# A graph network in twelve stages: steps further apart, byte flags, divided transfers, and two pieces of work in other stages

## The chip, the cores and the metric

The kernel runs on one core of one Trainium2 chip. A core has five engines, each with its own list of instructions: TensorE (PE in the profile; PEld is its loading of weights), VectorE (DVE), ScalarE (ACT), GpSimd (POOL) and SyncE (SP, which here only issues transfers), and sixteen DMA engines. The metric is the device time of one execution in microseconds (us); the profile also gives nanoseconds (ns) for single instructions.

## What is computed

x has 100000 nodes of 128 features; 50000 edges go from `src` (random) to `dst` (sorted). Four layers follow, each with a residual and a layer norm over the features. Cut to what matters:

```python
def _L0(x):     # attention per head (4 heads of 32)
    h = (x @ W).reshape(N, H, C)
    alpha = leaky_relu(s_src[row] + s_dst[col], 0.2)
    m = maximum(segment_max(alpha, row), 0.0); ex = exp(alpha - m[row])
    denom = segment_sum(ex, row) + (E - deg)[:, None] * exp(-m)
    return segment_sum((ex / denom[row])[:, :, None] * h[col], col) + bias
def _L1(x):     # attention over the edges of a receiver
    w = exp(e - m[receiver]);  e = sum(Q[receiver] * K[sender]) * scale
    attn = segment_sum(w * V[sender], receiver) / segment_sum(w, receiver)
    return x + attn @ Wo
def _L2(x):     # two graph convolutions; norm = dinv[dst] * dinv[src], with self loops
    for W, b in ((W0, b0), (W1, b1)):
        x = relu(segment_sum((x @ W)[src] * norm[:, None], dst) + b)
    return x
def _L3(x):     # messages of scalars and vectors; emb: 8 Gaussians of edge_weight
    w = mlp(emb); xs, xv = s @ W_up0, v @ W_up1
    mid = w * combinations(xs[src], xv[src], edge_attr_3 / norm(edge_attr_3))
    return segment_sum(mid, dst) @ W_out / 16
for layer in (_L0, _L1, _L2, _L3):
    x = layernorm(x + layer(x))
```

## The kernel before

`build` calls twelve stages one after the other, with a barrier of all engines between two: `prepare`, `scores_and_sort`, `gat_softmax`, `gat_sums`, `first_layer`, `radial_basis`, `attention_scores`, `attention_softmax`, `second_layer`, `gcn_first`, `gcn_second`, `final_edges`. Most stages run over the edges: 98 items of 4 x 128 edges (`ITEMS`), while `gat_softmax` also runs over all nodes (196 halves). A tile of an item is 128 partitions x 512 numbers; four buffers (`BUFS`) of each tile take turns.

The order of the work is written out by hand. `pipeline(engine, (f, lag), ...)` makes one engine's list: in slot q it does, in the order in which the parts stand, f for item q - lag. The engines aren't tied slot by slot. Each goes on as soon as what it waits for is there; `wait_item(engine, sems, t, u, back)` waits until a buffer of the item `back` earlier is free. A lag thus says how many items lie between two steps in an engine's list.

A sum over the edges of a receiver is made by turning the item with TensorE (edges to the free axis), a running sum along it on VectorE (`tensor_tensor_scan`), which goes on where the flag `cont` is 1 and begins anew where it is 0, and a multiplication by a weight matrix, which turns it back. The last edge of each receiver holds the sum. The scan of an item takes its start from the last column of the one before.

`prepare` loads the ids of the edges and the edge vectors, finds the flags (`same`, L377) and stores them as f32 in `t_cont`; the ids go from SBUF to `t_ids` (L281 to 284) and come back in another layout (L287). Each of the four scanning stages loads the 512 flags of its item for all partitions (`edge_line`, 256 KB).

`gat_softmax` (L937): GpSimd gathers scores (L978), the nodes run through the graph convolution without edges as a pipeline of 196 halves, VectorE then does the softmax over the sources in one go after `SPLIT` = 100 slots (L1088 on), GpSimd scatters the result (L985) while the pipeline goes on. `find_segments` (L860) finds where the segments of a list of ids begin and end; it needs four turns by TensorE (L857), one after the other. It is done for the sources there and for the targets in `gat_sums` (L1145), which then sums the attention over the receivers (`segment_scan`), stores the totals, loads them as rows and turns them. `radial_basis` (L2062) makes the eight Gaussians (`kept_emb`) for all edges from 8 loads of the weights, two VectorE operations, a square and an exponential on ScalarE, and a product.

The stages with loops over items, and their lists:

- `second_layer` (L1583): `weight` (GpSimd, L1629), `turn` (TensorE, L1646), `scan` (L1678), `multiply` (L1653), `add` with the measure of the norm (L1685, L1254 to 1268), `root` (ScalarE, L1277), `scale` (L1287, L1289), `widen` (GpSimd, L1634 to 1637: scale and shift times a factor of the node, for two outputs), `apply` (ScalarE, L1664, L1665), two stores.
- `gcn_first` (L1701) and `gcn_second` (L1795): four indirect gathers on GpSimd (L1724, L1822), `turn` of both the gathered and the own rows (L193, L194), `scan` (L1778, L1882), `multiply` (L1756, L1864; the second with a row of the bias times the degree's root, L1861), `take` or `add`, and the output. The second adds x2, which `second_layer` stored.
- `final_edges` (L1902): four gathers (L1960), `scale_x`, `turn_x`, `copy_x`, `project`, `messages`, `turn_sums`, `scan`, `reduce`, `combine`, `root`, `scale`, `apply`, four scatters to the output (L1952) `SCATTER_LAG` items after the gather.

## Time and profile before

| | |
|---|---|
| median of three runs | 7871.08 us (7854.48 to 7896.73) |
| the profiled execution | 7874.37 us, its span 7872.4 us |
| busy, share of the span | PE 51%, PEld 40%, DVE 45%, ACT 34%, POOL 48% |
| transfers | 1048.5 MB, mean 133 GB/s |
| mean granted TensorE clock | 0.672 of full speed |

The profile is of one execution. Busy times leave out register, branch, semaphore and DMA-issuing instructions, except that an indirect DMA counts on GpSimd, which makes it. A wait is put down to what released it; "issue" is time in which an engine waited for nothing that the profile shows, "remote" is a release whose instruction the profile does not name. The stages end at 94.7, 1384, 3340, 3489, 3897, 3957, 4650, 4686, 5375, 5973, 6590 and 7872 us.

### The profile page before, as it was taken

To read this page: it belongs to the slowest core of one execution; us is meant where nothing else is said; L and a number is where in the kernel's file an instruction comes from. 1 tells how busy PE (TensorE), PEld (TensorE's weight loads), DVE (VectorE), ACT (ScalarE), POOL (GpSimd) and SP (SyncE) were. 2 spreads that over 40 slices of the span, in tenths; PEclk is the share of its full clock that TensorE was granted. 3 is DMA by queue.
4 is the path that set the end of the run, shared out by engine and by line. 5 is a ranking of instruction groups with operands and counts; after the bars stand their busy time and mean duration, and the time that the engine had idled before them with its cause. 6 is when DMAs were issued, how large, how long until landed. Compare 5 with 4: busy or idle time off the path is not lost. (4 is left out here: it accounts for less than half of the span.)

```text
span 7872.4 us, 85274 instructions
## 1 busy us (share of the span) xinstructions
PE 4003.5 (51%) x18822; PEld 3174.7 (40%) x18822; DVE 3570.1 (45%) x12700; ACT 2687.6 (34%) x6766; POOL 3751.2 (48%) x4124
## 2 busy tenths in 40 slices
PE   2444444112961118825468764444556885555555
PEld 1443344101641015514356543333554554555554
DVE  4484444001671005548711135553334665656665
ACT  0014455001861018815433324442222332222222
POOL 3655655775006750003255532225665664666665
PEclk9655555555985559957789975556666666777676
DMA  1236666111851016624455547776777996333333
GB/s 51 64 89 184 185 191 188 36 19 48 262 174 34 21 39 216 216 64 132 110 132 151 158 129 193 190 192 155 178 180 183 220 218 150 98 101 98 101 98 79
DMA packets 1395766, 1048.50 MB, mean 133 GB/s; under 512 B 171017, under 2 KB 1232586, under 8 KB 1395521
## 3 DMA queue, kind: packets, MB, share of 16 engines
q1 hardware_dynamic: 1279294, 866.89, 39.6%
q0 software_dynamic: 112896, 179.36, 10.1%
q10 hardware_dynamic: 3458, 1.02, 0.1%
q14 instruction: 86, 0.70, 0.0%
q8 instruction: 32, 0.52, 0.0%
HBM read 603.60 MB, written 448.78 MB: 134 GB/s over the span
## 5 line engine op out<-in xcount | busy, mean ns | idle before, releaser
L985 POOL DMA_INDIRECT t_alpha<-gsm_raw,gsm_edge_idx x392 | 401.8, 1025 | 591.7 <-DVE gsm_raw L1107 467.2
L1128 PE MATMUL gsm_zr<-kept_ident,gsm_zT 128*128 128x128 f32 x784 | 141.0, 307 | 936.8 <-ACT gsm_zT L1030 749.4
L1952 POOL DMA_INDIRECT out_dram<-mss_o,kept_scat_idx x392 | 390.8, 997 | 364.6 <-ACT mss_o L1297 274.0
L511 POOL DMA_INDIRECT sort_xd<-in_x_dram,kept_dst_idx x392 | 378.6, 966 | 382.9 <-DMA t_xdst<-sort_xd 226.6
L1417 POOL DMA_INDIRECT asc_xs<-t_t,kept_idx_a x392 | 370.8, 946 | 354.2 <-issue 120.3
L1336 POOL TENSOR_TENSOR l_xb<-l_x,kept_bias 128x512 f32<-128x512 f32 x98 | 133.5, 1363 | 842.0 <-DMA l_x<-t_xdst 841.3
L741 PE MATMUL sort_sps<-kept_wa,sort_xdT 128*128 128x4 f32 x784 | 221.6, 353 | 607.0 <-ACT sort_xsT L765 572.8
L1128 PEld LDWEIGHTS gsm_zr<-kept_ident,gsm_zT 128*128 128x128 f32 x784 | 89.8, 150 | 986.9 <-ACT gsm_zT L1030 797.3
L1822 POOL DMA_INDIRECT gs_xs<-t_z,kept_idx_a x392 | 370.7, 946 | 237.0 <-issue 94.0
L1724 POOL DMA_INDIRECT gs_xs<-t_t,kept_idx_b x392 | 370.7, 946 | 214.6 <-issue 105.8
L978 POOL DMA_INDIRECT gsm_raw<-t_al,gsm_from_idx x392 | 395.6, 1009 | 161.5 <-issue 129.1
L1960 POOL DMA_INDIRECT mss_xs<-t_x,kept_idx_a x392 | 396.5, 1011 | 150.7 <-issue 119.2
L741 PEld LDWEIGHTS sort_sps<-kept_wa,sort_xdT 128*128 128x128 f32 x784 | 209.5, 327 | 641.0 <-ACT sort_xsT L765 400.3
L1070 DVE SCALAR_TENSOR_TENSOR gsm_y<-gsm_hp,gsm_x 128x512 f32<-128x512 f32 x196 | 135.5, 692 | 697.4 <-remote 569.3
L513 POOL DMA_INDIRECT sort_xs<-in_x_dram,kept_src_idx x392 | 379.4, 968 | 120.3 <-issue 119.9
L1297 ACT ACTIVATE mss_o<-mss_y,mss_nb,mss_rs 128x128 f32<-128x128 f32 x392 | 161.4, 482 | 756.7 <-DVE mss_nb L1289 451.1
L1030 ACT ACTIVATE gsm_zT<-gsm_zp,kept_b0col 128x512 f32<-128x512 f32 x196 | 134.7, 687 | 754.7 <-remote 477.2
L1511 DVE CUSTOM_DVE_ANT_0 asc_prod<-asc_qp,asc_xs 128x128 f32<-128x128 f32 x392 | 90.6, 287 | 557.3 <-remote 269.7
L1973 PE MATMUL mss_xtp<-kept_ident,mss_xk 128*128 128x128 f32 x392 | 106.1, 423 | 447.9 <-ACT mss_xk L2006 423.0
L1297 ACT ACTIVATE gsm_o<-gsm_y,gsm_nb,gsm_rs 128x128 f32<-128x128 f32 x784 | 323.2, 488 | 15.9 <-issue 15.6
L193 PE MATMUL gs_tp<-kept_ident,gs_xs 128*128 128x128 f32 x784 | 303.9, 394 | 46.3 <-issue 29.4
L1996 PE MATMUL mss_op<-kept_wout,mss_sc 128*128 128x128 f32 x1568 | 311.8, 383 | 4.0 <-DVE mss_sc L2045 4.0
(527 smaller groups left out, 12860.5 us busy)
## 6 DMA issues: line engine op xcount, KB each, us to landing
t_t<-sort_o SPq DMA_DIRECT2D x66, 792.0 KB
t_x<-gsm_o SPq DMA_DIRECT2D x196, 264.0 KB
sort_x<-in_x_dram SPq DMA_DIRECT2D x66, 768.0 KB
gsm_x<-t_t SPq DMA_DIRECT2D x196, 256.0 KB
t_z<-gsm_z SPq DMA_DIRECT2D x196, 256.0 KB
out_dram<-gsm_o SPq DMA_DIRECT2D x196, 256.0 KB
gs_cont<-t_cont SPq DMA_DIRECT2D x196, 256.0 KB
t_t<-l_o SPq DMA_DIRECT2D x98, 264.0 KB
```

The lines of the kernel that those rows point to most:

```text
L511: pool.indirect_dma_start(xd[u][:, j, :], None, A["x"], bass.IndirectOffsetOnAxis(K["dst_idx"][:, c:c + 1], 0)).then_inc(gathered[u], 16)
L513: pool.indirect_dma_start(xs[u][:, j, :], None, A["x"], bass.IndirectOffsetOnAxis(K["src_idx"][:, c:c + 1], 0)).then_inc(gathered[u], 16)
L741: pe.matmul(sps[:, j, 0:HEADS], xdT[u % 2][:, j, :], K["wa"][:, HEADS:8], start=True, stop=False)
L978: pool.indirect_dma_start(raw[:, c, 0:HEADS], None, T["al"], bass.IndirectOffsetOnAxis(from_idx[:, c:c + 1], 0)).then_inc(gathered[u], 16)
L985: pool.indirect_dma_start(T["alpha"], bass.IndirectOffsetOnAxis(edge_idx[:, c:c + 1], 0), raw[:, c, :], None).then_inc(scattered[u], 16)
L1297: ac = act.activation(norm["o"][u][:, g, :], norm["y"][u][:, g, :], ACT.Identity, bias=norm["nb"][u][:, g:g + 1], scale=norm["rs"][u][:, g ...
L1417: pool.indirect_dma_start(xs[u][:, j, :], None, T["t12"][0:EP + N], bass.IndirectOffsetOnAxis(K["idx_a"][:, c:c + 1], 0)).then_inc(gathere ...
L1724: pool.indirect_dma_start(xs[u][:, j, :], None, T["t12"], bass.IndirectOffsetOnAxis(K["idx_b"][:, c:c + 1], 0)).then_inc(gathered[u], 16)
L1822: pool.indirect_dma_start(xs[u][:, j, :], None, T["z1"], bass.IndirectOffsetOnAxis(K["idx_a"][:, c:c + 1], 0)).then_inc(gathered[u], 16)
L1952: pool.indirect_dma_start(T["out"], bass.IndirectOffsetOnAxis(K["scat_idx"][:, c:c + 1], 0), o[u][:, j, :], None, bounds_check=N - 1, oob_ ...
L1960: pool.indirect_dma_start(xs[u][:, j, :], None, T["x3"], bass.IndirectOffsetOnAxis(K["idx_a"][:, c:c + 1], 0)).then_inc(gathered[u], 16)
L1996: mm = pe.matmul(op[u % 2][:, j, :], sc[u][:, a, j * P:(j + 1) * P], K["wout"][:, a, :], start=(a == 0), stop=(a == parts - 1))
```

## The change

- `SCATTER_LAG` goes from 4 to 13, and the lags of `second_layer`, `gcn_first`, `gcn_second` and `final_edges` are larger, partly in another order within a slot.
- The flags are bytes. They are loaded once, in `gat_sums`, for all partitions (50176 bytes each) and stay in SBUF; the scans read them there.
- Transfers of 97 and 127 rows in `prepare` and `gat_sums` are divided into 96 + 1 and 112 + 15 rows. `prepare` loads the ids in the final layout, and `t_ids` is gone; the flags are found ahead of the norms of the vectors.
- Both `find_segments` run at the start of `gat_softmax`, ahead of its pipeline.
- The work of `radial_basis` is in `gat_sums`; the stage is gone.
- `second_layer` no longer stores x2. `gcn_second` reads the scaled rows that `second_layer` stored for `gcn_first` and puts the missing factor (1 / degree, `dinv2B`) on the product: four `Relu` activations on ScalarE (`lift`) read the product from PSUM, VectorE adds.

```diff
-SCATTER_LAG = 4
+SCATTER_LAG = 13
+EVEN_ROWS = E // (4 * P) // 16 * 16
...
-def edge_line(table, t, u):
-
-    return table[0:1, bass.ds(t * (4 * BUFS * P) + u * 4 * P, 4 * P)].broadcast_to([P, 4 * P])
+def goes_on(K, t, u):
+
+    return K["cont"][:, bass.ds(t * (4 * BUFS * P) + u * 4 * P, 4 * P)]
...
+            for a, (name, off) in enumerate([("dst", 0), ("dst", 1), ("src", 0)]):
...
+                sp.dma_start(ints[0:EVEN_ROWS, a, :],
+                             ids[off:off + EVEN_ROWS * 4 * P].rearrange("(p f) -> p f", f=4 * P)).then_inc(ids_loaded, 16)
+                sp.dma_start(ints[EVEN_ROWS:full_rows, a, :],
+                             ids[off + EVEN_ROWS * 4 * P:off + full_rows * 4 * P].rearrange("(p f) -> p f", f=4 * P)).then_inc(ids_loaded, 16)
...
-            for a in range(2):
-                sp.dma_start(T["ids"][a, 0:EP].rearrange("(p f) -> p f", f=CHUNKS), flts[:, a, :]).then_inc(ids_stored, 16)
...
-            for tile, a, off in [(cur, 1, 0), (nxt, 1, 1), (srow, 0, 0)]:
-                sp.dma_start(tile[0:rows].rearrange("p b i -> p (b i)"),
-                             T["ids"][a, off:off + EP].rearrange("(p f) -> p f", f=4 * P)).then_inc(rows_loaded, 16)
...
+            dve.wait_ge(ids_loaded, 144)
+            link(dve.tensor_copy(cur[:], ints[:, 0, :].rearrange("p (b i) -> p b i", b=4)))
+            link(dve.tensor_copy(nxt[:], ints[:, 1, :].rearrange("p (b i) -> p b i", b=4)))
+            link(dve.tensor_copy(srow[:], ints[:, 2, :].rearrange("p (b i) -> p b i", b=4)))
...
+            dve.tensor_copy(same8[0:rows], same[0:rows]).then_inc(same_ready, 1)
...
+def turn_by_tensor(pe, turner, ident, first=0, last=None):
+    for n in range(first, len(turner["turns"]) if last is None else last):
...
+            find_segments(dve, link, turner, seg, rec[:, 0, :])
+            dve.wait_ge(ids_loaded, 48)
+            link(dve.tensor_copy(ids[:], ids_int[:]))
+            find_segments(dve, link, turner, K["seg"], ids[:])
...
-            find_segments(dve, link, turner, seg, rec[:, 0, :])
...
+            turn_by_tensor(pe, turner, K["ident"], last=2 * FIND_TURNS)
             pipeline(pe, *parts, last=SPLIT)
-            turn_by_tensor(pe, turner, K["ident"])
+            turn_by_tensor(pe, turner, K["ident"], first=2 * FIND_TURNS)
...
-            sp.dma_start(raw[0:full].rearrange("p f h -> p (f h)"),
-                         T["alpha"][0:full * CHUNKS, :].rearrange("(p f) h -> p (f h)", f=CHUNKS)).then_inc(loaded, 16)
+            even = full // 16 * 16
+            sp.dma_start(raw[0:even].rearrange("p f h -> p (f h)"),
+                         T["alpha"][0:even * CHUNKS, :].rearrange("(p f) h -> p (f h)", f=CHUNKS)).then_inc(loaded, 16)
+            sp.dma_start(raw[even:full].rearrange("p f h -> p (f h)"),
+                         T["alpha"][even * CHUNKS:full * CHUNKS, :].rearrange("(p f) h -> p (f h)", f=CHUNKS)).then_inc(loaded, 16)
...
+            for g in range(8):
+                chunks = T["ew"].rearrange("a (t g i) -> a g t i", g=8, i=P)[:, g]
+                sp.dma_start(K["emb"][NB * g:NB * (g + 1)].rearrange("p (t i) -> p t i", i=P), chunks.broadcast_to([NB, EIGHTS, P])).then_inc(ew_loaded, 16)
+            for g in range(8):
+                sp.dma_start(K["m0g"][NB * g:NB * (g + 1), g, 0:64], A["L3_gnn_mlp_w0"]).then_inc(w_loaded, 16)
+            sp.dma_start(K["cont"][:], T["cont"][0:1, 0:EP].broadcast_to([P, EP])).then_inc(cont_loaded, 16)
...
+            link(dve.memset(K["emb"][:], 0.0))
+            dve.memset(K["m0g"][:], 0.0).then_inc(w_zero, 1)
...
-            find_segments(dve, link, turner, K["seg"], ids[:])
...
+            dve.wait_ge(ew_loaded, 128)
+            link(dve.tensor_scalar(inside[0:rows_r], flat, 1.0, None, ALU.is_le))
+            dve.tensor_scalar(flat, flat, 0.0, 1.0, ALU.max, ALU.min).then_inc(clipped, 1)
...
+            link(dve.tensor_tensor(K["dinv2B"][:], K["dinvB"][:], K["dinvB"][:], ALU.mult))
+            link(dve.tensor_scalar(K["degepsB"][:], K["dinv2B"][:], EPS * D, None, ALU.mult))
+            dve.wait_ge(expd, 1)
+            dve.scalar_tensor_tensor(out=flat, in0=flat, scalar=float(NB) ** 0.5, in1=inside[0:rows_r], op0=ALU.mult, op1=ALU.mult)
...
+            act.activation(flat, flat, ACT.Square, bias=center[0:rows_r, 0:1], scale=float(NB - 1)).then_inc(squared, 1)
...
+            act.activation(flat, flat, ACT.Exp, scale=-0.5).then_inc(expd, 1)
...
-                sp.dma_start(cont[u][:], edge_line(T["cont"], t, u)).then_inc(cont_loaded[u], 16)
...
-                sp.dma_start(edge_rows(T["x2"], t, u), o2[u][:]).then_inc(x_stored[u], 16)
-            pipeline(sp, (load, 0), (store, 5))
+            pipeline(sp, (load_xs, 0), (load_own, 3), (store, 10))
...
-                pool.tensor_tensor(rsx[u][:], norm["rs"][u][:], four(K["dsqrtB"], t, u), ALU.mult)
-                pool.tensor_tensor(nbx[u][:], norm["nb"][u][:], four(K["dsqrtB"], t, u), ALU.mult).then_inc(widened[u], 1)
-            pipeline(pool, (widen, 3), (weight, 0))
+                pool.tensor_tensor(nbz[u][:], norm["nb"][u][:], four(K["dlastB"], t, u), ALU.mult).then_inc(widened[u], 1)
+            pipeline(pool, (weight, 0), (widen, 6))
...
-            pipeline(pe, (multiply, 1), (turn, 0))
+            pipeline(pe, (multiply, 3), (turn, 1))
...
-                    act.activation(o[u][:, j, 0:D], y[u][:, j, :], ACT.Identity, bias=nbz[u][:, j:j + 1], scale=rsz[u][:, j:j + 1])
-                    ac = act.activation(o2[u][:, j, :], y[u][:, j, :], ACT.Identity, bias=nbx[u][:, j:j + 1], scale=rsx[u][:, j:j + 1])
+                for j in range(4):
+                    ac = act.activation(o[u][:, j, 0:D], y[u][:, j, :], ACT.Identity, bias=nbz[u][:, j:j + 1], scale=rsz[u][:, j:j + 1])
                 ac.then_inc(applied[u], 1)
...
-            pipeline(act, (apply, 4), (lambda t, u: norm_root(norm, act, t, u), 3))
+            pipeline(act, (lambda t, u: norm_root(norm, act, t, u), 5), (apply, 7))
...
-                dve.tensor_tensor_scan(sc[u][:], cont[u][:], tp[u % 2][:].rearrange("p j i -> p (j i)"),
+                dve.tensor_tensor_scan(sc[u][:], goes_on(K, t, u), tp[u % 2][:].rearrange("p j i -> p (j i)"),
...
-            pipeline(dve, (scan, 0), (add, 1), (scale, 2))
+            pipeline(dve, (scan, 2), (add, 4), (scale, 5))
...
-            pipeline(sp, (load, 0), (store, 3))
+            pipeline(sp, (load, 0), (store, 7))
...
-            pipeline(pe, (multiply, 1), (turn, 0))
+            pipeline(pe, (multiply, 2), (turn, 0))
...
-            pipeline(act, (activate, 2))
+            pipeline(act, (activate, 4))
...
-            pipeline(dve, (scan, 0), (take, 1))
+            pipeline(dve, (scan, 1), (take, 3))
...
+                sp.dma_start(x2[u][:], edge_rows(T["t12"][T12_Z:T12_Z + EP], t, u)[:, :, 0:D]).then_inc(x_loaded[u], 16)
...
+            pipeline(sp, (load_own, 0), (load_root, 1), (load_x, 3), (store, 9))
...
-                wait_item(pe, summed, t, u, 2)
+                wait_item(pe, lifted, t, u, 2)
...
-            pipeline(pe, (multiply, 1), (turn, 0))
+            pipeline(pe, (multiply, 2), (turn, 0))
...
+            def lift(t, u):
+                act.wait_ge(multiplied[u], t + 1)
+                wait_item(act, summed, t, u, 4)
+                for j in range(4):
+                    ac = act.activation(r[u][:, j, :], hp[u % 2][:, j, :], ACT.Relu, scale=K["dinv2B"][:, bass.ds(4 * BUFS * t + 4 * u + j, 1)])
+                ac.then_inc(lifted[u], 1)
...
-            pipeline(act, (lambda t, u: norm_apply(norm, act, t, u, stored), 3), (lambda t, u: norm_root(norm, act, t, u, bias=K["zero"]), 2))
+            pipeline(act, (lambda t, u: norm_root(norm, act, t, u, bias=K["zero"]), 5), (lift, 3), (lambda t, u: norm_apply(norm, act, t, u, stored), 6))
...
-                dve.scalar_tensor_tensor(out=y[u][:], in0=hp[u % 2][:], scalar=0.0, in1=x2[u][:],
-                                         op0=ALU.max, op1=ALU.add).then_inc(summed[u], 1)
+                dve.tensor_tensor(y[u][:], r[u][:], x2[u][:], ALU.add).then_inc(summed[u], 1)
...
-            pipeline(dve, (scan, 0), (add, 1), (lambda t, u: norm_scale(norm, dve, t, u), 2))
+            pipeline(dve, (scan, 1), (add, 4), (lambda t, u: norm_scale(norm, dve, t, u), 5))
...
-            pipeline(sp, (load, 0), (load_y, 2))
+            pipeline(sp, (load, 0), (load_y, 5))
...
-            pipeline(pe, (reduce, 2), (turn_sums, 1), (turn_x, 0), (project, 0))
+            pipeline(pe, (turn_x, 1), (reduce, 7), (project, 3), (turn_sums, 5))
...
-            pipeline(act, (lambda t, u: norm_apply(norm, act, t, u, scattered, 64), 4), (lambda t, u: norm_root(norm, act, t, u), 3),
-                     (scale_x, 0), (copy_x, 0))
+            pipeline(act, (copy_x, 2), (lambda t, u: norm_root(norm, act, t, u), 9), (scale_x, 0),
+                     (lambda t, u: norm_apply(norm, act, t, u, scattered, 64), 10))
...
-            pipeline(dve, (scan, 1), (messages, 0), (combine, 2), (lambda t, u: norm_scale(norm, dve, t, u), 3))
...
+            pipeline(dve, (scan, 6), (messages, 4), (combine, 8), (lambda t, u: norm_scale(norm, dve, t, u), 9))
...
-    T["cont"] = dram("t_cont", (1, EP + P))
+    T["cont"] = dram("t_cont", (1, EP + P), mybir.dt.uint8)
...
+            if stage is gat_sums:
+                K["cont"] = sb("cont", [P, EP], mybir.dt.uint8)
+                sb_radial = stage_makers(nc, radial, "kept")[0]
+                K["m0g"] = sb_radial("m0g", [P, 8, P])
+                K["emb"] = sb_radial("emb", [P, EIGHTS * P])
             stage(nc, A, T, K)
```

## Rows read from the trace of the kernel before

**Rows 1.** Busy time by stretch: columns in the header, clock and DMA share last.

```profile
core 0: us, PE busy (x) PEld busy (x) DVE busy (x) ACT busy (x) POOL busy (x), PEclk, DMA share, GB/s
0.00:95.00 95.00, 10.55 (x38) 7.08 (x38) 28.99 (x60) 2.16 (x2) 0.70 (x6) 1.00 0.13 38
...
1384.00:1900.00 516.00, 79.12 (x230) 48.90 (x230) 30.52 (x149) 38.20 (x89) 384.87 (x381) 0.54 0.13 23
1900.00:2290.00 390.00, 322.49 (x1726) 214.40 (x1727) 238.62 (x1214) 307.68 (x780) 10.71 (x12) 0.94 0.76 235
...
3340.00:3489.00 149.00, 14.56 (x58) 8.90 (x56) 57.02 (x133) 9.94 (x26) 0.00 (x0) 0.54 0.14 50
...
3897.00:3957.00 60.00, 0.00 (x0) 0.00 (x0) 20.03 (x7) 12.23 (x3) 0.13 (x1) 0.50 0.31 30
...
4686.00:5375.00 689.00, 312.18 (x1176) 244.72 (x1176) 356.39 (x1279) 331.99 (x883) 161.41 (x490) 0.50 0.73 188
5375.00:5973.00 598.00, 324.20 (x1568) 291.46 (x1568) 225.73 (x491) 125.27 (x392) 370.74 (x392) 0.68 0.70 173
5973.00:6590.00 617.00, 489.36 (x1764) 340.16 (x1764) 377.82 (x1378) 179.90 (x490) 370.74 (x392) 0.63 0.89 210
6590.00:7872.00 1282.00, 708.46 (x3528) 630.72 (x3528) 753.88 (x2157) 353.93 (x980) 787.25 (x784) 0.70 0.37 97
```

**Rows 2.** Waits in second_layer: waiter, releaser, us in all, times, longest.

```profile
POOL ats_rsz L1634 <- DVE ats_nb L1289: 512.3, 98, 7.2
...
DVE ats_sc L1678 <- PE ats_tp L1646: 300.8, 98, 4.5
```

**Rows 3.** Timeline inside second_layer: start, us, engine, line, instruction, idle before.

```profile
5002.48 1.28 DVE L1678 TENSOR_TENSOR_SCAN ats_sc<-ats_cont,ats_sc,ats_tp 128x512 f32<-128x512 f32 x1 [3.03 <-PE ats_tp L1646]
...
5003.81 2.07 PE L1653 MATMUL ats_hp<-kept_wvo,ats_sc 128*128 128x128 f32 x8 [1.37 <-DVE ats_sc L1678]
...
5008.14 1.11 PE L1646 MATMUL ats_tp<-kept_ident,ats_xw 128*128 128x128 f32 x4 [2.25 <-POOL ats_xw L1629]
...
5009.29 1.28 DVE L1678 TENSOR_TENSOR_SCAN ats_sc<-ats_cont,ats_sc,ats_tp 128x512 f32<-128x512 f32 x1 [3.01 <-PE ats_tp L1646]
```

**Rows 4.** The page's costliest groups, gathers of both graph convolutions: busy, mean ns, idle.

```profile
L1822 POOL DMA_INDIRECT gs_xs<-t_z,kept_idx_a x392 | 370.7, 946 | 237.0 <-issue 94.0
L1724 POOL DMA_INDIRECT gs_xs<-t_t,kept_idx_b x392 | 370.7, 946 | 214.6 <-issue 105.8
```

**Rows 5.** The same list, gathers and scatters of final_edges.

```profile
L1952 POOL DMA_INDIRECT out_dram<-mss_o,kept_scat_idx x392 | 390.8, 997 | 364.6 <-ACT mss_o L1297 274.0
...
L1960 POOL DMA_INDIRECT mss_xs<-t_x,kept_idx_a x392 | 396.5, 1011 | 150.7 <-issue 119.2
```

**Rows 6.** Waits in the gather phase of gat_softmax (1384 to 1885 us).

```profile
PE gsm_zr L1128 <- ACT gsm_zT L1030: 366.5, 10, 42.9
DVE gsm_y L1070 <- remote: 306.7, 9, 35.6
```

**Rows 7.** The same wait of TensorE in the stretch after it (1900 to 2290 us).

```profile
PE gsm_zr L1128 <- ACT gsm_zT L1030: 72.2, 87, 42.9
```

**Rows 8.** A wait of VectorE in attention_scores (3957 to 4650 us).

```profile
DVE asc_prod L1511 <- remote: 269.7, 31, 20.0
```

**Rows 9.** A wait of VectorE in gat_sums (3340 to 3490 us).

```profile
DVE gsu_v L1192 <- DMA gsu_raw<-t_alpha: 58.2, 1, 58.2
```

**Rows 10.** Timeline of gat_softmax, first instruction of find_segments and the one after it.

```profile
2297.27 0.06 DVE L863 MEMSET gsm_src_cont<- 128x1 f32 x1
...
2307.99 4.00 DVE L901 TENSOR_TENSOR_SCAN gsm_run<-gsm_src_negcont,gsm_al 128x392 f32<-128x392 f32 x4
```

**Rows 11.** Waits of VectorE in prepare (0 to 96 us).

```profile
DVE prep_flts L361 <- DMA prep_ew<-in_edge_weight_dram: 27.7, 1, 27.7
DVE prep_sq L365 <- DMA prep_vec<-in_edge_attr_dram: 21.8, 1, 21.8
```

229 lines of the change are left out of this document (94 added, 135 removed).

## The prediction

> **What bounds the kernel now.** I read first the busy time by stretch, one stretch a stage [rows 1]: no engine is busy for much more than half of the whole, so the bound has to be found stage by stage. In `second_layer` (689 us for 98 items) the busiest engine, VectorE, has 356.39 us of work. In the two graph convolutions (598 and 617 us) GpSimd and TensorE are busiest, in `final_edges` (1282 us) GpSimd with 787.25 us. None fills its stage. Then I read the waits and the timeline of each.
>
> `second_layer` is a closed loop through four engines. One item takes 6.81 us, from scan to scan (5002.48 to 9.29) [rows 3]. GpSimd waits 512.3 us for VectorE's scale of an older item before it may weight the next one (its list puts `widen` ahead of `weight`), and VectorE waits 300.8 us for TensorE's turn of that weighted item [rows 2]. This is order, not work.
>
> `gcn_first` and `gcn_second` need 6.1 and 6.3 us an item. The four indirect gathers of an item cost GpSimd 4 x 0.946 us, and the pause between two that it spends issuing is 119.2 / 392 = 0.30 us in the nearest row, so 4 x 1.25 = 5.0 us is its floor [rows 4, 5]. Before, TensorE multiplies item q-1 ahead of turning item q, and the scan of q-1 stands between two turns: turn, scan (1.28), multiply, turn.
>
> `final_edges` takes 13.1 us an item with fill and drain. GpSimd's eight indirect transfers an item cost 4 x 1.011 + 4 x 0.997 + 8 x 0.30 = 10.4 us; 274.0 us it waits for ScalarE's result, which is to be scattered only four items after its gather [rows 5].
>
> One phenomenon of this trace speaks to all of it. While GpSimd issues indirect transfers back to back, results of TensorE reach the other engines late. In the gather phase of `gat_softmax`, where GpSimd never waits, VectorE waits up to 35.6 us for a product, nine times, and TensorE 366.5 us for ScalarE [rows 6]; ten items pass in 500 us. In the next stretch, without gathers, 87 pass in 390 us, about 4.2 us each once the first wait is over [rows 1, 7]. In `attention_scores` such late signals still hold VectorE for 269.7 us over 98 items, 2.75 us each [rows 8].
>
> **The change, part by part.** The sum stands against the profiled execution, 7874.4 us (its span is 7872.4), 3 us above the median of 7871.1.
>
> *second_layer.* The second output (four ScalarE activations, two small GpSimd multiplies, a 256 KB store) and the 256 KB flag load go; 1288 KB an item become 776. `weight` comes first on GpSimd and `widen` six items later, TensorE multiplies two items after turning. The loop is cut, and what is left is the busiest engine: VectorE 356.39 / 98 = 3.64 us plus its small gaps, 3.85; TensorE at the granted 0.50 clock 1.11 + 2.07 plus two handovers, about 3.6 [rows 1, 3]. DMA: 188 GB/s at a share of 0.73 is 257 GB/s full, so 776 KB take 3.1 us. I take 4.1 us an item, 98 x (6.81 - 4.1) = 266, less 6 for deeper filling: 260. Bounds: 3.85 us (285) and 4.6 us, one more handover of the size of the shown gaps (210). GpSimd issues no indirect transfers here, so the late signals have no place.
>
> *gcn_first, gcn_second.* Two items now lie between turn and multiply, the flag load goes (1024 to 768 KB an item, about 1288 to 1032). In `gcn_second` the root of the degree moves from the stored x2 into four activations an item on ScalarE. Eight an item and a root take 331.99 us in `second_layer`, so four more are some 160; ScalarE has 179.90 of 617 now and stays free. TensorE has there 489.36 / 98 = 5.0 us of work at 0.63 clock and stays close behind the 5.0 of GpSimd [rows 1]. Reaching the floor would give 598 - (98 x 5.1 + 15) = 83 and 617 - 515 = 102 us. Nothing at all is the other bound: every stage of this trace that issues gathers stays at least 1 us an item above its floor. I take about half the way, 5.5 to 5.7 us: 45 and 40.
>
> *final_edges.* Everything moves apart (scatter 13 items after gather, apply 10), so the wait of 274.0 us can go; VectorE's 753.88 / 98 = 7.7 and TensorE's 7.2 us fit under GpSimd's 10.4 [rows 1, 5]. Late next is GpSimd itself. All of the wait gone would leave 98 x 10.5 + 35 = 1064, a gain of 218; if a pause of 1.5 us an item remains, it is 70. I take 11.0 us an item: 160. The longer drain (13 items of scatters alone, 5.2 us each, 68 us) runs beside the chain of the last items, which is what ended the stage before too, and costs nothing as long as that chain is no shorter than 68 us; if it is shorter, up to 20 us.
>
> *gat_softmax.* `find_segments` of the sources leaves the stretch in which all wait for VectorE: 2307.99 - 2297.27 = 10.7 us [rows 10]. It and the one for the targets now run before the pipeline, in the gather phase. Each has four turns through TensorE, eight in series, and the node pipeline stands behind them on TensorE and VectorE. Were all eight late by 35.6 us [rows 6] they would take 285 us, in which the pipeline did five items before; those are made up later at 4.2 us each, 21 us. The loss is 0 if the turns come on time and at most all ten items, 42. I take 20: net 9 us worse (11 better to 31 worse).
>
> *gat_sums and radial_basis.* VectorE waits 58.2 us for a 1.6 MB load of 127 rows [rows 9]. As 112 + 15 rows I take 6 us, 1.6 MB at the 257 GB/s from above: 52. The target segments go: 10.7, by [rows 10]. The stage of the basis, 60 us, goes [rows 1]; of its 20.03 us VectorE and 12.23 us ScalarE, the clears (6) stand ahead of the wait, the compare and clip (7) lie partly under the stores of the totals, the exponential and the last product (13) end the stage, beside index work of about 5. The flags, 6.4 MB for all partitions, are loaded in the same queue ahead of those stores: 25 us at 257 GB/s, of which about 10 come out on the path. So 52 + 11 - 6 - 2 - 10 - 10 = 35 (10 to 50), and 60. Of the split the nearest row gives no size: zero is the lower bound, 58 the upper.
> The Trainium skill speaks on both sides of that split. "DMA: Bandwidth & Descriptors", section "Why a DMA increments its semaphore by 16 and not by 1", spreads a transfer over the largest divisor up to 16 of its slowest dimension: 127 rows go to one engine, 112 to sixteen. By that rule the wait ends under the clears. The same page's "Rules for kernel authors" advises against dividing a transfer by partitions because the parts share the same engines; by that alone nothing is gained, and the time would be some 60 us longer. The size of the wait, 1.6 MB in about 60 us or 27 GB/s against 257, agrees with the first.
>
> *prepare* (95 us). VectorE waits 27.7 us for the ids and the weights, and 21.8 for the vectors [rows 11], of odd row counts; the ids then made a way through memory. Directly loaded, even rows: 25 (10 to 40).
>
> Sum: 260 + 45 + 40 + 160 - 9 + 35 + 60 + 25 = 616; 7874.4 - 616 - 3 = 7255, given as 7250. With all low bounds 210 + 0 + 0 + 50 - 31 + 10 + 60 + 10 = 309 (7562), all high 285 + 83 + 102 + 218 + 11 + 50 + 60 + 40 = 849 (7022).
>
> **The rivals.**
> A: the distance does all it can, and every loop stage comes down to its busiest engine: the high sum, about 7040. For it: those engines have no other wait than the ones that the distance removes. Against it: no gathering stage here does so. Chance 0.17.
> B: late TensorE signals, not the order, set the gathering stages. GpSimd pauses only when its four buffers are full, the signals pass in the pause, and one pause an item of 1.0 to 1.5 us stays: 5.0 + 1.1 = 6.1 is just what `gcn_first` takes. Then the convolutions gain nothing, `final_edges` 70, the moved segments cost 31 - 11 = 20: 260 + 70 - 20 + 35 + 60 + 25 = 430, about 7440. Chance 0.19.
> C, the other side: with the waits gone GpSimd pauses so seldom that the signals starve. By the price of `attention_scores`, 2.75 us an item [rows 8], on the 294 items of the three gathering stages that is 809 us more; the other parts give 371. The time would be about 8310. It decides from 371 / 294 = 1.26 us an item on. Against it: four buffers of gathers are at most 20 us (in `final_edges` 42) of uninterrupted issue. Chance 0.03.
> D: the byte flags don't do what they say: no scan of the trace reads bytes. If a scan of 1.28 us took twice that, `second_layer` would be bound by VectorE at 5.1 us (98 us lost) and `final_edges` by VectorE at 7.7 + 2.6 = 10.3 us beside GpSimd (some 50): about 7400. Chance 0.04. With less, nothing comes out.
>
> **How the numbers follow.** Forecast 0.55 (its own range 7120 to 7380), A 0.17, B 0.19, D 0.04, C 0.03; 0.02 for a sum that a wait not thought of cancels. The range 7030 to 7460 takes in A and B and leaves out C and the tails. A measurement of this kernel can tell about 0.5% (39 us) from no change. Faster 0.95, within 0.5% 0.02, slower 0.03.
>
> **What the profile after would show.** `second_layer` near 430 us with VectorE busy over 80%, no wait of GpSimd for VectorE: right. The convolutions at 5.5 to 5.7 us an item; at 6.1 B is right, at 5.1 A. GpSimd's wait for ScalarE in `final_edges` under 80 us and the stage at 1120; if instead TensorE's results are marked late by 5 us and more, it is B or C. Scans of 1.28 us refute D. The wait for the 127 rows at under 8 us; fewer than ten items in the gather phase. The prediction is wrong above all if the gathering stages (together 245 us of the sum) behave otherwise than half way.

## The result, and the profile after

The changed kernel takes 7505.41 us (median of four executions, 7501.45 to 7515.43) against 7880.42 us before: a ratio of 0.9529, 95% interval 0.9499 to 0.9559. The forecast was 7250 us, 7030 to 7460; the measured time lies above the range. The profiled execution has a span of 7499.4 us.

Stage by stage (from a stage's first instruction to the next stage's first, us, and for `final_edges` to its own last; by this measure the `gat_sums` of the kernel before begins at 3355.4 us and not at 3340; the last two columns are from runs 13 and 14, further down, on another chip):

| stage | before | changed | difference | forecast | before, chip 15 | changed, chip 15 |
|---|---|---|---|---|---|---|
| prepare | 94.4 | 58.9 | -35.5 | -25 | 93.9 | 59.1 |
| scores_and_sort | 1289.0 | 1287.5 | -1.5 | 0 | 1042.6 | 1038.3 |
| gat_softmax | 1971.1 | 1969.8 | -1.3 | +9 | 1091.3 | 1081.1 |
| gat_sums | 134.0 | 96.7 | -37.3 | -35 | 133.4 | 96.4 |
| first_layer | 410.3 | 410.5 | +0.2 | 0 | 411.6 | 413.7 |
| radial_basis | 57.4 | gone | -57.4 | -60 | 57.4 | gone |
| attention_scores | 693.6 | 697.4 | +3.8 | 0 | 499.9 | 499.9 |
| attention_softmax | 35.8 | 35.2 | -0.6 | 0 | 35.8 | 35.3 |
| second_layer | 689.1 | 402.8 | -286.3 | -260 | 688.5 | 403.2 |
| gcn_first | 597.8 | 592.1 | -5.7 | -45 | 503.0 | 503.2 |
| gcn_second | 618.1 | 616.7 | -1.4 | -40 | 561.5 | 528.8 |
| final_edges | 1279.9 | 1330.1 | +50.2 | -160 | 1273.5 | 1017.6 |

So the parts outside the gathering stages came as forecast or a little better, and the three gathering stages lost 43 us where 245 were to be gained. The busy time by stretch of the changed kernel answers to [rows 1] (columns as there):

```profile
0.00:59.00 59.00, 10.54 (x38) 7.08 (x38) 30.62 (x62) 2.16 (x2) 0.70 (x6) 1.00 0.18 45
1347.00:1850.00 503.00, 69.76 (x198) 42.06 (x198) 41.51 (x181) 31.13 (x72) 375.26 (x373) 0.53 0.12 22
3317.00:3414.00 97.00, 7.83 (x28) 5.17 (x28) 63.83 (x82) 13.48 (x5) 0.13 (x1) 0.52 0.51 127
4557.00:4959.00 402.00, 206.86 (x1176) 177.84 (x1176) 357.53 (x1275) 181.18 (x491) 132.97 (x294) 0.77 0.74 194
4960.00:5551.00 591.00, 302.58 (x1568) 285.76 (x1568) 222.15 (x491) 125.03 (x392) 370.57 (x392) 0.68 0.51 132
5552.00:6168.00 616.00, 432.47 (x1764) 302.67 (x1764) 376.68 (x1374) 282.31 (x882) 398.98 (x392) 0.71 0.65 169
6168.00:7498.00 1330.00, 547.03 (x3528) 508.25 (x3528) 743.25 (x2157) 348.50 (x980) 772.49 (x784) 0.70 0.28 74
```

VectorE works 357.53 us of 402 in `second_layer`, 89%. In `final_edges` no engine is busy for longer than before, and the stage takes longer. The waits of the changed kernel in `final_edges` (waiter, releaser, us in all, times, longest us):

```profile
ACT mss_xsT L2058 <- remote: 672.8, 46, 22.1
...
PE mss_xtp L2019 <- ACT mss_xsT L2058: 495.9, 38, 21.0
...
POOL out_dram L1998 <- ACT mss_o L1352: 292.4, 50, 12.9
```

The first line is ScalarE's copy of a turned item (`copy_x`). It waits 672.8 us, up to 22.1 us at once, where the same copy before waited 131.5 us (117.8 for its turn and 13.7 "remote"). Its list makes it wait for two results of TensorE, the turn of its item and the product (`project`) of the item two before. By the trace's own record of the semaphores the product came last in 74 of the 89 waits over 1 us. GpSimd's wait for ScalarE, 274.0 us before [rows 5], is 292.4 us still. How a late result looks, in the changed `gcn_first` (start, us, engine, line, instruction, idle before):

```profile
5210.74 0.42 PE L195 MATMUL gs_tp<-kept_ident,gs_own 128*128 128x128 f32 x1
...
5213.61 0.27 PE L195 MATMUL gs_tp<-kept_ident,gs_own 128*128 128x128 f32 x1
5213.85 0.95 POOL L1768 DMA_INDIRECT gs_xs<-t_t,kept_idx_b  x1 [0.30 <-issue]
5216.73 1.28 DVE L1820 TENSOR_TENSOR_SCAN gs_sc<-kept_cont,gs_sc,gs_tp 128x512 f32<-128x512 f32 x1 [7.27 <-DMA asm_rows<-t_w]
5216.86 0.94 POOL L1768 DMA_INDIRECT gs_xs<-t_t,kept_idx_b  x1 [2.06 <-DMA asm_rows<-t_w]
...
5218.95 1.27 DVE L1820 TENSOR_TENSOR_SCAN gs_sc<-kept_cont,gs_sc,gs_tp 128x512 f32<-128x512 f32 x1
```

TensorE ends the last turn of one item at 5211.16 and that of the next at 5213.88. The first scan shown waits for the earlier of the two and starts at 5216.73, 5.6 us after it; the second, at 5218.95, belongs to the later one. GpSimd's last indirect transfer ends at 5214.80, and GpSimd then stands still for 2.06 us; the first scan starts 1.93 us into this pause. The releaser that the profile names for the scan, a DMA of another stage, can't be the one: the tiles of that DMA have nothing to do with the scan.

The trace also records when a semaphore was raised, which the views don't print. TensorE's semaphore for the turn that ended at 5211.16 was raised at 5216.60, and that for the turn of 5213.88 at 5216.79. Over the whole of the changed `gcn_first` the median time from the end of a TensorE instruction to its semaphore is 4.7 us (185 records); for ScalarE and VectorE in the same stage it is 0.01 us. So it is TensorE's signals that come late, and no other compute engine's.

### The profile page after: what moved, and what is told of

Its sections match the earlier page's. It is cut to its first block and busy times, and to the rows that moved or that the text cites. A ratio compares the mean times of both kernels' runs of the same rounds, so it can differ in the third digit from the quotient of the medians.

```text
span 7499.4 us, 83670 instructions
## 1 busy us (share of the span) xinstructions
PE 3661.2 (49%) x18822; PEld 2946.9 (39%) x18822; DVE 3560.4 (47%) x12705; ACT 2634.2 (35%) x6767; POOL 3733.9 (50%) x3928
## 5 line engine op out<-in xcount | busy, mean ns | idle before, releaser
L1998 POOL DMA_INDIRECT out_dram<-mss_o,kept_scat_idx x392 | 392.6, 1002 | 415.5 <-ACT mss_o L1352 292.4
L1865 POOL DMA_INDIRECT gs_xs<-t_z,kept_idx_a x392 | 399.0, 1018 | 204.6 <-issue 106.6
L2006 POOL DMA_INDIRECT mss_xs<-t_x,kept_idx_a x392 | 379.8, 969 | 166.9 <-issue 117.4
L2090 DVE TENSOR_TENSOR_SCAN mss_sc<-kept_cont,mss_sc,mss_tp 128x512 f32<-128x512 f32 (+1 forms) x196 | 240.2, 1267 | 453.2 <-DMA t_x<-gs_o 445.3
L2019 PE MATMUL mss_xtp<-kept_ident,mss_xk 128*128 128x128 f32 x392 | 84.7, 356 | 584.0 <-ACT mss_xsT L2058 495.9
L2058 ACT COPY mss_xsT<-mss_xtp 128x512 f32<-128x512 f32 x98 | 57.4, 586 | 795.3 <-remote 672.8
L1352 ACT ACTIVATE sort_o<-sort_x,sort_nb,sort_rs 128x128 f32<-128x128 f32 x792 | 312.1, 487 | 0.0
```

The lines of the kernel that those rows point to most:

```text
L1352: ac = act.activation(norm["o"][u][:, g, :], norm["y"][u][:, g, :], ACT.Identity, bias=norm["nb"][u][:, g:g + 1], scale=norm["rs"][u][:, g ...
L1865: pool.indirect_dma_start(xs[u][:, j, :], None, T["z1"], bass.IndirectOffsetOnAxis(K["idx_a"][:, c:c + 1], 0)).then_inc(gathered[u], 16)
L1998: pool.indirect_dma_start(T["out"], bass.IndirectOffsetOnAxis(K["scat_idx"][:, c:c + 1], 0), o[u][:, j, :], None, bounds_check=N - 1, oob_ ...
L2006: pool.indirect_dma_start(xs[u][:, j, :], None, T["x3"], bass.IndirectOffsetOnAxis(K["idx_a"][:, c:c + 1], 0)).then_inc(gathered[u], 16)
L2090: sn = dve.tensor_tensor_scan(sc[u][:, a, :], goes_on(K, t, u), tp[:, a].rearrange("p j i -> p (j i)"), sc[(u - 1) % BUFS][:, a, 4 * P - 1 ...
```

## The experiments

Theory H: while GpSimd issues indirect transfers one after another, results of TensorE reach the other engines only when GpSimd pauses, and a greater distance lets GpSimd run on for longer. Rival O: the order within the new lists costs by itself. Rival G: the gathered data come late. A third possibility is that any busy GpSimd does it. Runs 2 to 7, 10, 13 and 18 are single executions, so they carry no interval; the executions of one kernel on one chip differ by at most 0.6%, and what is read from the single ones, stage by stage, is larger. The stage times of all of them, in us (g = `gcn_first`, h = `gcn_second`, f = `final_edges`; "ops" are multiplications of 128x392 numbers on GpSimd into tiles that nobody reads):

| run | kernel | second_layer | g | h | f |
|---|---|---|---|---|---|
| 1 | old lags | 657.8 | 590.7 | 609.2 | 1278.8 |
| 2 | plain transfers | 403.3 | 245.0 | 436.6 | 814.5 |
| 3 | plain transfers, old lags | 658.1 | 358.1 | 493.0 | 1245.3 |
| 4 | GpSimd waits for its gathers | 403.4 | 765.3 | 696.0 | 1257.5 |
| 5 | plain transfers, GpSimd does ops | 403.7 | 313.6 | 592.6 | 1093.8 |
| 6 | plain transfers, unread gathers | 403.8 | 583.7 | 605.9 | 1324.3 |
| 7 | one op an item in g and h, two in f | 403.1 | 583.3 | 609.0 | 1183.3 |
| 10 | as 7, old lags in g, h and f | 403.3 | 588.0 | 613.0 | 1471.8 |

**Run 1, the old lags.** In the changed kernel:

```diff
-SCATTER_LAG = 13
+SCATTER_LAG = 4
...
-            pipeline(pe, (turn_x, 1), (reduce, 7), (project, 3), (turn_sums, 5))
+            pipeline(pe, (reduce, 2), (turn_sums, 1), (turn_x, 0), (project, 0))
```

and likewise for the lists of the other engines and of the other three stages.

> The changed kernel with the lags and list orders of the kernel before in second_layer, gcn_first, gcn_second and final_edges; the byte flags, the missing x2 store and all the rest stay as changed. Theory H (results of TensorE are held back while GpSimd issues indirect transfers, and the greater distance lets GpSimd run on for longer without a pause): final_edges returns to about 1280 us from 1330, the two convolutions stay within 10 us of 592 and 617, second_layer goes back towards 600 to 690; the whole 7505 - 50 + 200 to 290 = 7650 to 7750. Rival O (the new order inside final_edges costs by itself, for instance through the single buffer between turn_x and copy_x, and signals have nothing to do with it): the same 1280 for final_edges, but the convolutions, whose order got looser, should be 20 to 60 us slower than in the changed kernel. For second_layer: if the distance made the gain, it is at 650 or more; if the removed store and applications made it, near 400.

Measured: 7652.59 us, ratio 0.9773 (0.9756 to 0.9789). `final_edges` returns to 1278.8, so its loss comes from the distances and not from the byte flags. The convolutions don't move (1.4 and 7.5 us less): the distance is worth nothing there. `second_layer` is at 657.8: of its 286 us, 255 are the distance and 31 the removed output and flag load.

**Runs 2 and 3, plain transfers.** The four gathers of an item become one load of consecutive rows by SyncE, the scatters a plain store (for this the load of y comes two items later and the store stands at 11):

```diff
-                    pool.indirect_dma_start(xs[u][:, j, :], None, T["t12"],
-                                            bass.IndirectOffsetOnAxis(K["idx_b"][:, c:c + 1], 0)).then_inc(gathered[u], 16)
+                sp.dma_start(xs[u][:], edge_rows(T["t12"][T12_Z:T12_Z + EP], t, u)).then_inc(gathered[u], 16)
```

> The changed kernel in which gcn_first, gcn_second and final_edges take consecutive rows by plain loads from SyncE's queue in place of the indirect gathers, and final_edges stores consecutive rows in place of its scatters; GpSimd has nothing to do in the three stages (the output is therefore another one). Theory H: without indirect transfers TensorE's signals are on time, and with the new distances the stages come down to their busiest engine: gcn_first about 400 us, gcn_second 480 to 520, final_edges 850 to 950. Rival O: final_edges stays over 1200, since its own order binds it.

> The plain loads and stores of the run before, with the lags and orders of the kernel before in the four stages. Theory H: slower than with the new distances in each of the three stages (the distance is worth something once signals are on time): gcn_first 500 or more against 400, gcn_second 560 against 500, final_edges 1100 to 1200 against 900. Rival O: final_edges is faster here than with the new order.

Busy time by stretch of the three stages, run 2 and then run 3:

```profile
4917.00:5161.00 244.00, 207.76 (x1568) 179.83 (x1568) 223.29 (x490) 125.11 (x392) 0.00 (x0) 0.98 1.10 319
5162.00:5597.00 435.00, 367.91 (x1764) 253.88 (x1764) 374.59 (x1374) 280.38 (x882) 0.00 (x0) 0.80 0.93 239
5598.00:6413.00 815.00, 524.22 (x3528) 494.76 (x3528) 741.58 (x2157) 352.21 (x980) 0.00 (x0) 0.84 0.45 127
```

```profile
5167.00:5524.00 357.00, 205.27 (x1568) 181.14 (x1568) 225.60 (x491) 125.28 (x392) 0.00 (x0) 0.97 0.82 218
5525.00:6017.00 492.00, 427.25 (x1764) 294.19 (x1764) 375.02 (x1375) 286.81 (x882) 0.00 (x0) 0.71 0.78 211
6018.00:7263.00 1245.00, 705.70 (x3528) 628.07 (x3528) 751.81 (x2157) 351.92 (x980) 0.00 (x0) 0.70 0.31 83
```

With GpSimd at rest the new distances give 358.1 to 245.0, 493.0 to 436.6 and 1245.3 to 814.5 us: 113, 56 and 431. With the gathers they give nothing, nothing and a loss of 51. The new order is therefore not what costs, and O falls. Part of this is TensorE's clock: it is much the same in `gcn_first` (0.97 and 0.98), but 0.70 with the old lags against 0.84 in `final_edges`, and 0.71 against 0.80 in `gcn_second`. The times that I had expected with the new distances were too long (400, 480 and 850). With the old lags those of the convolutions were too long as well, by 142 and 67, and that of `final_edges` (1100 to 1200) too short by 45. The loop of `gcn_first` takes 3.6 us an item at this clock. In run 2 TensorE's signals are on time, by a median of 0.01 us in each of the three stages. Its `gcn_first` moves 319 GB/s, the changed kernel's 132, so the load of the DMA engines isn't what makes them late.

**Run 4, a pause.** One line after the gathers of an item, in all three stages:

```diff
+                    pool.wait_ge(gathered[u], 64 * t + 64)
```

> The changed kernel in which GpSimd, after the four gathers of an item, waits until they have landed (three stages); this adds a pause of about 2 us an item to the engine with the most work. Theory H: the pause lets held signals pass, so final_edges becomes faster in spite of it, 1220 to 1290 against 1330; TensorE's results reach the others within about 3 us. The convolutions: GpSimd's 5.0 us and a pause of 2 make 7 us an item at worst, 690, at best no change. Rival O, and any theory in which GpSimd's work bounds: every stage longer by up to 98 x 2 = 196 us.

`final_edges` gets 73 us faster although GpSimd is made to wait in each item. `gcn_first` was outside the expectation: 7.8 us an item, 0.8 more than the worst that I had named. The pause there is longer than 2 us. `gcn_second`, 696.0, is 6 us over the worst, and the whole takes 7643.94 us, longer than the changed kernel.

**Runs 5 and 6, what of GpSimd does it.** Both stand on run 2. In run 5 GpSimd does 4, 4 and 8 ops an item; in run 6 it does as many indirect gathers into tiles that no step reads:

```diff
+                for j in range(4):
+                    c = 4 * q + j % 4
+                    pool.indirect_dma_start(dx[u][:, j, :], None, T["t12"],
+                                            bass.IndirectOffsetOnAxis(K["idx_b"][:, c:c + 1], 0)).then_inc(fetched[u], 16)
```

> As e2_plain (consecutive rows by plain loads and stores in gcn_first, gcn_second and final_edges, another output), and GpSimd does 4, 4 and 8 multiplications of 128x392 numbers an item into scratch tiles, paced as its gathers were: a busy GpSimd without indirect transfers. If only indirect transfers hold TensorE's signals (H): the stages stay near 245, 437 and 815 us or at GpSimd's own time for the operations where that is longer (about 1 us each: 4 us an item or 400 us, and 8 us or 800), without late signals. If any busy GpSimd holds them (H2): back towards 590, 617 and over 1200.

> As e2_plain, and GpSimd issues four, four and eight indirect gathers an item into tiles that nobody reads (the output is that of e2_plain); no step of the pipelines waits for one. H: these transfers alone bring the stages back: gcn_first and gcn_second to 570 to 620 us, final_edges to 1200 to 1330, where GpSimd's own floor is 490, 490 and 1020. If what is slow about the indirect gathers is that their data come late (rival G), the stages stay where GpSimd's pace puts them, 490 to 520 and 1020 to 1060, as nothing but the pace of GpSimd reaches the others, or lower for the parts that don't depend on it.

Run 6 decides it: 583.7, 605.9 and 1324.3 us, the changed kernel's 592.1, 616.7 and 1330.1 within 11 us, though no step needs a gathered row. G falls. Its stretches:

```profile
4934.00:5516.00 582.00, 291.69 (x1568) 277.09 (x1568) 221.88 (x490) 125.02 (x392) 369.61 (x392) 0.71 0.68 180
5517.00:6122.00 605.00, 439.66 (x1764) 306.05 (x1764) 377.40 (x1374) 282.20 (x882) 398.97 (x392) 0.69 0.84 214
6123.00:7447.00 1324.00, 566.61 (x3528) 526.22 (x3528) 744.24 (x2157) 353.40 (x980) 745.23 (x784) 0.69 0.45 118
```

What this leaves open is whether GpSimd's issuing of these transfers does it or the transfers once they are under way; no run parts the two.

In run 5 GpSimd works without a break in `gcn_first` (312.20 us of 313), and no late result is left (median 0.01 us; in run 6 it is 4.4 us there), but the stages aren't at run 2's times, which I had expected of `gcn_second` and `final_edges`. There it is VectorE itself that got slower. Two of its operations in `gcn_second`, run 2 and then run 5 (busy us, mean ns of one):

```profile
L1921 DVE TENSOR_TENSOR gs_y<-gs_r,gs_x 128x512 f32<-128x512 f32 x98 | 65.4, 667 | 0.0
...
L1325 DVE TENSOR_TENSOR gs_mv<-gs_mv,gs_diff 128x4 f32<-128x4 f32 x98 | 16.0, 163 | 3.3
```

```profile
L1947 DVE TENSOR_TENSOR gs_y<-gs_r,gs_x 128x512 f32<-128x512 f32 x98 | 90.3, 921 | 0.0
...
L1325 DVE TENSOR_TENSOR gs_mv<-gs_mv,gs_diff 128x4 f32<-128x4 f32 x98 | 40.0, 408 | 3.4
```

The same 128x4 operation takes 408 ns beside GpSimd's ops and 163 without, the addition 921 and 667; VectorE's work in the stage is 534.52 us where it was 374.59. The Trainium skill, "SBUF — State Buffer", under "Terms", has GpSimd and VectorE arbitrate for one pair of ports that one of them holds for a whole instruction. The trace agrees for these operations. The scans, which read one operand from PSUM, kept their 1.28 us.

**Runs 7, 8 and 10, a gap in place of a wait.**

```diff
+                    if 2 * q + 0 > 3:
+                        pool.wait_ge(worked, 2 * q + 0 - 3)
+                    pool.tensor_tensor(scr[(2 * q + 0) % 4][:], K["rhatB"][:, 0, 0:392], K["rhatB"][:, 0, 0:392], ALU.mult).then_inc(worked, 1)
...
```

> The changed kernel with one multiplication of 128x392 numbers on GpSimd after the four gathers of an item in the two convolutions, two in final_edges (about 1 us each). If signals pass whenever GpSimd is not issuing an indirect transfer for over a microsecond (H, a break need not be idle): final_edges 1180 to 1290 against 1330, the convolutions within 20 us of 592 and 617 or up to 50 slower. If only an idle GpSimd lets them pass: all three slower, final_edges 1400 and more.

> The changed kernel in which GpSimd waits for its gathers to land in final_edges alone. H: final_edges about 1258 us as in e4_pause, all else as in the changed kernel: 0.9% to 1.0% under the changed kernel, that is a ratio to the kernel before of 0.943 to 0.945 where the changed kernel has 0.953. A theory in which GpSimd's work bounds the stage: slower than the changed kernel.

> The changed kernel with the old lags in the two convolutions and in final_edges, and with the operations on GpSimd as in e7_pool_op (one an item in the convolutions, two in final_edges). It says what the distance is worth once held results pass. H: final_edges 1250 to 1290 us, against 1183 with the new distances and the same operations, and against 1279 with the old lags and without them; the convolutions 590 to 640. If the gap alone makes the gain and the distance nothing: final_edges 1183.

Run 7 took 7293.69 us, with the same indirect transfers and with work added to the engine that has most of it. GpSimd's timeline in its `final_edges`:

```profile
6705.16 0.94 POOL L2021 DMA_INDIRECT mss_xs<-t_x,kept_idx_a  x1 [0.30 <-issue]
6706.12 0.86 POOL L2025 TENSOR_TENSOR mss_scr<-kept_rhatB 128x392 f32<-128x392 f32 x1
6706.91 0.85 POOL L2028 TENSOR_TENSOR mss_scr<-kept_rhatB 128x392 f32<-128x392 f32 x1
6707.93 1.03 POOL L2013 DMA_INDIRECT out_dram<-mss_o,kept_scat_idx  x1 [0.17 <-issue]
```

and its waits there:

```profile
POOL mss_xs L2021 <- issue: 117.3, 391, 0.3
...
POOL out_dram L2013 <- ACT mss_o L1352: 21.9, 5, 12.6
```

The gap between two transfers is 6707.93 - 6706.10 = 1.8 us. GpSimd's wait for ScalarE is down from 292.4 to 21.9 us; the engine is now the bound, 12.1 us an item. The convolutions of this run have one op an item, a gap of 1.03 us. One such gap in `gcn_first`, and the only wait of GpSimd of over 10 us in that stage:

```profile
5203.69 0.94 POOL L1771 DMA_INDIRECT gs_xs<-t_t,kept_idx_b  x1 [0.30 <-issue]
5204.64 0.86 POOL L1775 TENSOR_TENSOR gs_scr<-kept_rhatB 128x392 f32<-128x392 f32 x1
5205.66 0.98 POOL L1771 DMA_INDIRECT gs_xs<-t_t,kept_idx_b  x1 [0.16 <-issue]
```

```profile
POOL gs_xs L1771 <- issue: 103.8, 382, 0.5
```

GpSimd no longer waits for the pipeline there, which it did for 98 us in the changed kernel (74.2 and 23.5 us, put down to two DMAs), and the stage takes 583.3 us. TensorE's signals are no less late than before (median 5.3 us), but they pass once an item, in time. Run 8 (the wait of run 4 in `final_edges` alone) took 7378.73 us, ratio 0.9413 (0.9388 to 0.9437), a little under the expected 0.943: 1257.6 us in the stage. Run 10 shows what the distance is for: with the old lags the same ops make `final_edges` 1471.8 us, 193 longer than without them, 1.97 us an item where the gap is 1.83. That reads as if the gap stood whole in a closed loop; this was argued and not tested. I had expected 1250 to 1290. The distance is worth 289 us with gaps and minus 51 without.

**Runs 9 and 11, gaps in all gathering stages.** The same two ops after each item in `scores_and_sort`, both phases of `gat_softmax` and `final_edges`, after each second in `attention_scores` and the convolutions; run 11 halves them except in `gat_softmax`.

> The changed kernel with two multiplications of 128x392 numbers on GpSimd (a gap of about 1.7 us between two indirect transfers) after each item in scores_and_sort, in the gather and the scatter phase of gat_softmax and in final_edges, after every second item in attention_scores and the two convolutions. H: every gap lets TensorE's held results pass. gat_softmax: its node pipeline makes 40 halves and more in a phase that goes from 500 to 670 us, where it made nine, so the stage goes from 1970 to 1650 to 1800 us; scores_and_sort from 1288 to 1180 to 1250; attention_scores and the convolutions within 30 us of 670, 592 and 617, final_edges 1183 as in e7_pool_op. The whole 6900 to 7150, a ratio of 0.88 to 0.91. If the gaps help only where GpSimd waits for the pipeline: gat_softmax longer by up to 340 us and the whole over 7500.

> As e9_pool_ops_everywhere with half as many gaps in scores_and_sort, attention_scores, the two convolutions and final_edges (gat_softmax as there). It tells whether the number of gaps or GpSimd's own work sets these stages. If GpSimd's work does: the convolutions lose 0.43 us an item, 584 to 540 and 610 to 570, final_edges 1187 to 1110, the sort 1200 to 1120. If the number of gaps does: they go back towards the changed kernel, 590, 615, 1330 and 1288. Taken between, since held results wait twice as long: convolutions unchanged, final_edges 1200 to 1260, the sort 1220 to 1260, the whole 6650 to 6750.

Run 9: 6619.99 us, ratio 0.8438 (0.8422 to 0.8454), faster than both kernels and 280 us faster than I had expected. `gat_softmax` takes 1381.1 us in place of 1969.8, where I had 1650 to 1800. Its gather phase, which answers to the second row of [rows 1], and TensorE's wait there, which answers to [rows 6]:

```profile
1260.00:1930.00 670.00, 386.38 (x1982) 253.93 (x1982) 428.56 (x1470) 349.94 (x876) 535.52 (x588) 0.85 0.54 157
```

```profile
PE gsm_zr L1168 <- ACT gsm_zT L1066: 88.5, 61, 2.9
```

The phase is 670 us long and not 503 as in the changed kernel, but TensorE does 386 us of work in it where it did 70, and its longest wait there is 2.9 us and not 42.2. GpSimd waits there for nothing but its issuing once it has begun. Run 11: 6825.78 us, ratio 0.8703 (0.8679 to 0.8726); `scores_and_sort` 1283.2 us against 1199.5 and `final_edges` 1261.1 against 1186.9. GpSimd's own work is less in run 11, and the stages are slower. In `final_edges` GpSimd waits 164.7 us for ScalarE again, where it waited 25.5 in run 9. So with all the gaps GpSimd's work is the bound, and with half of them the held results cost time again. I had expected less of a step: 1220 to 1260 for the sort and 6650 to 6750 for the whole, both missed, and 1200 to 1260 for `final_edges`, missed by 1.

**What is left of H.** That TensorE's signals come late beside indirect transfers is shown (runs 2, 5 and 6 and the semaphores). That they pass only when GpSimd pauses is not. In the changed `final_edges` 155 of TensorE's signals are over 1.5 us late; 110 of them pass while GpSimd stands still for over 0.5 us, 45 while it goes on issuing. One of these, ScalarE's copy, after 12.09 us:

```profile
6712.44 0.95 POOL L2006 DMA_INDIRECT mss_xs<-t_x,kept_idx_a  x1 [0.30 <-issue]
6713.56 0.59 ACT L2058 COPY mss_xsT<-mss_xtp 128x512 f32<-128x512 f32 x1 [12.09 <-remote]
6713.69 0.94 POOL L2006 DMA_INDIRECT mss_xs<-t_x,kept_idx_a  x1 [0.30 <-issue]
```

In the gather phase of `gat_softmax` GpSimd never pauses, and the signals pass all the same, some of them over 50 us late. Nor are they late from the start. GpSimd issues there without a break from 1352.55, and those of TensorE's signals that the trace records up to 1378.48 come within 0.01 us:

```profile
1357.05 0.28 DVE L880 COPY gsm_src_r_first<-gsm_turn_out 5x128 f32<-5x128 f32 x1 [0.57 <-PE gsm_turn_out L863]
```

The first late one is raised at 1388.00, 7.8 us late, and the next are 33 and 50 us late. A pause lets held signals pass sooner; what makes them late, and what frees them without a pause, is open.

**Runs 12 to 18, another chip.** Run 12 has one op after each item everywhere.

> One multiplication on GpSimd after every item in all six stages: gaps of about 1.0 us in place of 1.9. In scores_and_sort and final_edges GpSimd does as much in all as in e11_half_the_ops, in shorter gaps twice as often. In the traces held results pass about 1.3 us after the end of GpSimd's last indirect transfer; if a gap has to be that long, gaps of 1.0 us do little: final_edges 1260 to 1330, the sort 1280, gat_softmax 1700 to 1970, the whole over 7000. If any gap passes the results: final_edges 1110 to 1187, the sort 1100 to 1200, gat_softmax 1330 to 1400, the whole under 6600.

It took 6217.77 us, but the kernel before took 6399.43 us beside it, where it had taken 7830 to 7880 in all comparisons until then. Runs 1 to 11 ran on chips 2, 10 and 12, run 12 on chip 8; the chip of the first comparison is not on record. Runs 13 to 16 put four kernels on one chip (15).

> The kernel before, traced on the chip of this comparison. On a chip that holds TensorE's results back (C1): about 7840 us, the stages as in the document. On one that doesn't (C2), as the chip of e12_short_gaps, where the kernel before took 6399 us: every TensorE result at once, the sort near 1000 to 1050 us, gat_softmax 1200, the convolutions 490 to 520, final_edges 1150 to 1280.

> The changed kernel on the chip of this comparison. C1: a ratio of 0.953 to 0.960. C2: my forecast of the parts without held results should hold: second_layer 403 against 690, final_edges at GpSimd's floor, 1030 to 1060 us, the convolutions near 500, together 0.88 to 0.92 of the kernel before, that is 5650 to 5900 us.

> e9_pool_ops_everywhere again. C1: 6620 us, a ratio of 0.84. C2: the operations cost GpSimd 1.7 us an item and give nothing back, so it is slower than the changed kernel by 98 x 1.7 = 170 us in the sort and in final_edges, by 83 in the convolutions and in attention_scores: about 6350 us.

> e12_short_gaps again. C1: decides what the run on the other chip could not: 7000 us and more if a gap of 1.0 us is too short for held results to pass, under 6600 if any gap passes them. C2: 6218 us, a ratio of 0.97, and slower than the changed kernel.

Measured: before 6396.47 us, changed 5681.63 (ratio 0.8883, 0.8868 to 0.8898), the gaps of run 9 6522.81 (1.0196, 1.0179 to 1.0213), those of run 12 6218.28 (0.9721, 0.9705 to 0.9737). The kernel before on this chip, its gather phase in `gat_softmax`, `gcn_first` and `final_edges`:

```profile
1137.00:1620.00 483.00, 368.15 (x1970) 244.31 (x1970) 271.91 (x1377) 347.25 (x876) 361.06 (x383) 0.91 0.74 218
4055.00:4558.00 503.00, 285.77 (x1568) 246.76 (x1568) 225.69 (x491) 125.23 (x392) 369.88 (x392) 0.72 0.79 206
...
5120.00:6394.00 1274.00, 705.40 (x3528) 626.96 (x3528) 753.80 (x2157) 353.95 (x980) 782.93 (x784) 0.70 0.37 97
```

and the changed kernel, the gather phase, `gcn_first` and `final_edges`, with GpSimd's waits in the last:

```profile
1098.00:1575.00 477.00, 371.22 (x1978) 245.39 (x1978) 288.92 (x1437) 347.49 (x876) 356.66 (x378) 0.95 0.75 221
...
3628.00:4131.00 503.00, 278.57 (x1568) 255.84 (x1568) 225.72 (x496) 125.00 (x392) 369.97 (x392) 0.77 0.61 155
...
4660.00:5678.00 1018.00, 587.78 (x3528) 562.85 (x3528) 743.96 (x2157) 343.84 (x980) 770.19 (x784) 0.76 0.36 97
```

```profile
POOL mss_xs L2006 <- issue: 118.9, 390, 0.3
POOL out_dram L1998 <- issue: 117.8, 387, 0.3
```

In the gather phase of the kernel before TensorE does 368 us of work beside GpSimd's transfers, with no gap put in; on the first chip it did 79. TensorE's signals are on time here, by a median of 0.01 us in every gathering stage of runs 13 and 14. The changed `final_edges` is at GpSimd's own 10.4 us an item: it waits for nothing but its issuing. On chip 15 the gaps give nothing back: I had expected 6350 us for run 15, and it is 173 longer, since the gaps in `gat_softmax`, which my sum left out, cost 300 us (1381.1 against 1081.1). Of run 13 I had `gat_softmax` too long (1200 against 1091.3) and `gcn_second` too short (at most 520 against 561.5).

One comparison across the chips says most about the gaps. With those of run 9 the two kinds of chips take nearly the same time: `gat_softmax` 1381.1 us on both, `scores_and_sort` 1199.5 and 1190.1, `gcn_first` 583.8 and 582.3, `gcn_second` 610.4 and 610.7, `final_edges` 1186.9 and 1173.8; only `attention_scores` keeps a difference of 70 us (647.2 and 577.3). Without gaps the changed kernel needs 7505 us on the one kind and 5682 on the other.

Runs 17 and 18 were to decide whether short gaps work where results are held, and fell on chip 6, which holds none.

> e12_short_gaps once more, beside e9 on one chip. On a chip that holds results back (the kernel before at about 7840 us): 7000 us and more if a gap of 1.0 us is too short for held results to pass, under 6600 if any gap passes them. On one that doesn't: 6218 us again.

> e9_pool_ops_everywhere for comparison: 6620 us on a chip that holds results back, 6523 on one that doesn't.

They took 6216.96 and 6520.67 us (before 6401.0). The changed kernel's ratio in run 14 lies in the expected 0.88 to 0.92. As a whole, the kernel with the short gaps never ran on a chip that holds results back. Of the convolutions more can be said: run 7 has just these gaps there, on chip 10, which does hold them, and takes 583.3 and 609.0 us, against 581.7 and 616.7 in run 16 on chip 15. A gap of 1.0 us an item is enough for these two stages. For `scores_and_sort`, `gat_softmax` and `final_edges` it stays open. So chips 2, 10 and 12 held TensorE's results back, chips 6, 8 and 15 did not, each the same in all its executions. The comparisons of the second kind are also the later ones, so a difference of the chips and one of the time can't be told apart here.

## Why the prediction was wrong, point by point

The kernel saves 375 us where 616 was forecast. The parts outside the three gathering stages gave some 45 more than their 371; the step that failed is the worth of the distance in the gathering stages, 245 of the sum and 43 lost instead. I took their waits for order, which distance removes, and they were TensorE's late signals, which it doesn't.

- **second_layer** (260): right, 286 measured, 1 over the upper bound that I gave. The period is 3.9 us from scan to scan and VectorE the bound. Distance 255, less work 31 (run 1). One sign failed: GpSimd still waits 252.9 us for VectorE, 98 times, which costs nothing, as GpSimd isn't the bound.
- **gcn_first, gcn_second** (45, 40): wrong on the chip of the result, 6 and 1. The step that failed here is the closed loop that I read from the lists (turn, scan, multiply, turn) and half of whose loss I took back. Its own length in `gcn_first` is 3.6 us an item at clock 0.97 (run 3), and on chip 15, at 0.72, it still fits beside GpSimd's transfers: 503 us are 5.1 an item. So in `gcn_first` it didn't bind. What stood between 5.0 and 6.1 us was the held results (runs 2, 3 and 6; on chip 15, without them, the kernel before takes 5.1), and the distance doesn't touch them. On chip 15 `gcn_first` stands at its floor before and after, 503, so the 45 us weren't there to be gained on either kind of chip. In `gcn_second` the order does cost something: GpSimd waits 57.9 us for TensorE in run 13, and 33 us are gained.
- **final_edges** (160): wrong in sign, 50 slower. I took the wait of 274.0 us [rows 5] as a matter of order and let a small rest remain. It is a wait of 292.4 us still, in 50 pieces of 5.8 us in place of 95 of 2.9: GpSimd runs on further without a pause, TensorE's results are held for as long, and nothing is gained by its being ahead. By the semaphores, 53 of 362 recorded signals of TensorE were over 1.5 us late in this stage before, by a median of 2.6 us; in the changed kernel 155 of 384 are, by 15.4 us. On chip 15 the step holds as it was argued: the wait goes, the floor is reached, and 256 us are gained, 38 more than my upper bound. I had put the floor at 10.5 us an item and 35 us for fill and drain; the whole stage takes 10.4 an item.
- **The two rivals about held results.** B named the mechanism and gave 7440, 65 us under the result. It had the convolutions right (nothing); in `final_edges` it let 70 be gained where 50 were lost, and the 65 us are small partly because its other parts were too low. C named the starving as well, priced by the 2.75 us of [rows 8], and that price was too high: the stage lost 0.5 us an item, the convolutions nothing. Even `attention_scores` itself is only 194 us longer than on chip 15 (693.6 and 499.9), 2.0 us an item. I gave the two 0.22 together. The rows on which they stood [rows 6, 8] were the same as for the forecast, and they were the strongest of the trace; the forecast met them with "half way", for which no row spoke.
- **gat_softmax** (9 worse): 1 better. The eight turns came on time, as the line at 1357.05 above shows for the first: both `find_segments` are over 29 us after the stage's start, and seven halves passed in place of ten [rows 6]. The loss was three halves, some 13 us at 4.2 each, not the five that I took, and the 10.7 us of the sources' segments stand against it. TensorE's wait in the phase:

```profile
PE gsm_zr L1147 <- ACT gsm_zT L1045: 295.5, 7, 42.2
```

- **gat_sums, radial_basis, prepare** (35, 60, 25): 37, 57, 36. The wait of 58.2 us [rows 9] is gone altogether, as the Trainium skill, "DMA: Bandwidth & Descriptors", section "Why a DMA increments its semaphore by 16 and not by 1", would have it, and not the advice against dividing under "Rules for kernel authors". No run divides the load alone, so this rests on the changed kernel's trace. TensorE's wait for the totals, whose stores stand behind the flags and the loads of the basis in SyncE's queue, went from 16.3 to 33.1 us: 17 more, where I had 10.
- **D, the byte flags**: refuted. The scan of `final_edges` takes 1267 ns as before.
- The sum on chip 15 is 715 us where 616 was forecast. That it lies within the bounds of the sum, 309 to 849, is partly luck: `final_edges` gave 96 more than forecast and `gcn_first` 45 less. The argument for `final_edges` held on a chip on which results come on time, and the trace that it was made from showed that they didn't.

## What to carry to other kernels

Ahead of giving steps more distance, see in the trace whether the engines' results arrive when they end. If an engine waits long after its producer's last instruction ended, and mostly starts when GpSimd pauses, distance buys nothing and can cost. Gaps of 1.8 us between groups of indirect transfers took the changed kernel from 7505 to 6620 us here (run 9; as ratios to the kernel before beside them, 0.953 and 0.844). The same gap cost 841 us on a chip that holds nothing back (runs 14 and 15), so such a measure has to be timed on more than one chip. And a closed loop that is read from a list should be given its own length before its removal is priced: if it is shorter than the work of the busiest engine, it isn't what binds.

## What of the hardware was not expected

- On three of six chips engines waited up to some 20 us in `final_edges` and 40 us in `gat_softmax` for TensorE's results while GpSimd issued indirect transfers, and on three they did not. Only TensorE's signals were late (median 4.7 us in the changed `gcn_first`); ScalarE's and VectorE's came within 0.01 us. The kernel before takes 7830 to 7880 us on the ones and 6396 to 6401 on the others. Indirect transfers do it (run 6), tensor work on GpSimd does not (run 5). For the first 26 us of uninterrupted issuing in `gat_softmax` the signals were on time. The mechanism is open.
- Two multiplications between transfers, 1.8 us, let results pass, and bring both kinds of chips to nearly the same time in five of the six stages with gaps (runs 9 and 15). A gap of 1.0 us an item did as much in the two convolutions (run 7); elsewhere that was not settled.
- GpSimd's multiplications make some of VectorE's small operations more than twice as long, 163 to 408 ns (runs 2 and 5); others, such as the statistics of the norm (281 ns), stay as they were.
